# Routing a block every four to five shared-expert chunks and moving five blocks' shared products into the last stage of a ViT-tower kernel

## The chip, the cores and the metric

One NeuronCore of one Trainium2 chip runs the whole program. The metric is the device time of one launch in microseconds, given as the median of several runs. TensorE is written PE below, VectorE DVE, ScalarE ACT, GpSimd POOL and SyncE SP; PEld is PE's loading of weights, which overlaps its products. A name with q (SPq, ACTq) is that engine issuing a DMA.

## The reference, cut to what matters

```python
h = tok(x, ...)                  # real 2-D FFT of 16x16 patches, projection, class token, positions
h = h + ssm(layernorm(h), ...)   # causal convolution of each channel with a kernel of 197 taps
h = h + ffn(layernorm(h), ...)
def ffn(x):                      # 64 images x 197 tokens, width D = 192
    gates, idx = top_k(softmax(x @ router_w), 2)     # 8 experts, 2 for each token
    gates = gates / sum(gates)
    routed = sum over the 2 experts of gate * (silu(x @ w_gate[e]) * (x @ w_up[e])) @ w_down[e]
    shared = (silu(x @ ws_gate) * (x @ ws_up)) @ ws_down       # hidden width 768
    alpha = sigmoid(x @ sg_w + sg_b)
    return alpha * shared + (1 - alpha) * routed
```

All is float32 outside. Inside, the products of the FFN are made of float16 halves: each number is the sum of a high half and a low half (scaled by 16 for the weights), and a product is three to five products of halves.

## The kernel before, in words

`build` (L1697) runs five stages, one after the other, with a barrier between each and the next: `embed`, `mix`, and the three of `feed_forward`: `shared_expert`, `routed_experts`, `combine`.

**embed** (L148) reads the pixels, makes the 12608 token rows, stores them in `resid` and keeps their norm in the tile `u`. Beside that it makes the taps of the convolution: DVE raises powers step by step (`chain` and `raised`, most of whose instructions stand at the helper's line L433) into the tiles `zq` (14 powers) and `zp` (15), and PE multiplies them (`tap_products`, L384) in groups 5 to 10 of the 16 groups of images. `zp` already has its power index innermost in memory; `zq` has the channel innermost, and PE's moving operand reads it with a permuted pattern.

**mix** (L627) is the convolution. Its result lies in `y`; the last part of it is stored to `mixed` in DRAM by ACT's queue as the stage ends (`y_stored`).

**shared_expert** (L747) works on 25 blocks of 512 tokens (the last has 384). Two things happen for each block.
- *Routing* of a block: `add` (DVE: `resid` plus `mixed` into `sums`, then norm statistics, L1164 to L1173), `rstd` (POOL, L1111 and L1113), `normal` (DVE, L1179), `x_high` (ACT, L1039), `x_low` (POOL, L1117 and L1118), `transposes` (PE, 12 products, L943), `x_out` (ACT, L1044 and L1048, into `xt`), `router` (PE, 20 small products, L955), `logits` (DVE, L1191 to L1212), `tanh` (ACT), `ranks` (PE, L965 and L967), `slots` (DVE, L1218 to L1248), `send` (POOL, 8 indirect DMAs that scatter the token rows to `routed` by expert, L1128).
- *Shared products* of a block: six chunks m = 0..5 of 128 hidden units. For a chunk PE does `up` (10 products of 512 columns, L978, into `psg` and `psu`), ACT `silu` (L1059), DVE `hidden` (L1299), ACT `high` (L1067), DVE `low` (L1306), PE `down` (12 products of 192 columns, L992). After the six, DVE adds the block to `sums` (`token_out`, L1313).

The order on every engine is written out by hand in `body` functions. PE does `up` of a chunk and then `down` of the chunk two before it; both `psg`/`psu` and the hidden tiles have two buffers, so `up` of chunk c waits for `hidden` of c-2, and `down` of c-2 for `low` of c-2. Block b+1 is routed while block b's products run, each step at a fixed chunk of b: DVE has `add` at m = 0, `token_out` and `normal` at m = 1, `logits` at 4, `slots` at 5; ACT `x_high` at 2, `x_out` at 3; PE `transposes` at 3, `router` at 4, `ranks` at 5. `transposes` waits for `x_low` (and for `slots` of the block before). The FFN weights come in 12 pieces (`stage_in` on SP, `stage_high` on ACT, `stage_low` on DVE): four ahead of the first block, three in block 0, five in the last two. SP's queue starts with seven loads of constants (L877), then two pieces, then waits for `y_stored` and loads blocks 0 and 1 (one `hin` and four `yin` DMAs each). After the last block DVE works out the table of units (`unit_table`, L1250), and SP then stores eight blocks of filler rows at addresses that this table's first step gives (L925).

**routed_experts** (L1363) goes through 52 units of 512 rows. Its first load is SP's L1434, and its results are scattered to `parts`.

**combine** (L1640): for each block SP loads two parts (L1664), through a ring of six buffers; DVE adds one and then the other to `sums` (L1674, L1678); ACT's queue stores the block to `out` (L1694). PE and POOL do nothing.

Of the kernel before, what the change touches and what calls it, by code (L numbers as in the profile page):

```python
# [25 lines left out]
D = 192  # L26
# [52 lines left out]
NU = 60  # L79
MAX_UNITS = 2 * NTOK // UNIT + E  # L80
# [67 lines left out]
def embed(nc, io, u, area, taps, resid, mixed):  # L148

    with ExitStack() as ctx:  # L150
# [9 lines left out]
        zq, = pieces_of(free[1], ((2, KB, DH),))  # L160
# [112 lines left out]
        def _(act):  # L273
# [42 lines left out]
            for step in range(NG + 3):  # L316
# [56 lines left out]
        def _(pe):  # L373
# [11 lines left out]
            def tap_products(g, m):  # L385
# [325 lines left out]
def feed_forward(nc, io, area, y_stored, resid, mixed, routed, parts, out):  # L711

    with ExitStack() as ctx:
        t = {"w": [ctx.enter_context(nc.sbuf_tensor(f"ffn_w_{n}", [128, W_COLS], F16)) for n in ("hi", "lo")],
             "ident": ctx.enter_context(nc.sbuf_tensor("ident", [128, 128], F16)),
             "units": ctx.enter_context(nc.sbuf_tensor("units", [128, 2, NU], U32)),
             "expert": ctx.enter_context(nc.sbuf_tensor("expert", [128, NU], F32)),
             "pairs": ctx.enter_context(nc.sbuf_tensor("pairs", [128, 1], U32)),
             "sums": (ctx.enter_context(nc.sbuf_tensor("sums", [128, NTILE - HELD, D], F32)),
                      area[:, 0:HELD * D].rearrange("p (t d) -> p t d", d=D))}  # L720
        shared_expert(nc, io, t, area, y_stored, resid, mixed, routed, out)
        routed_experts(nc, t, routed, parts)
        combine(nc, t, parts, out)
# [23 lines left out]
def shared_expert(nc, io, t, area, y_stored, resid, mixed, routed, out):  # L747


    with ExitStack() as ctx:  # L750
# [7 lines left out]
        wa = [x[:, 0:2 * HS].rearrange("p (k h) -> p k h", k=2) for x in w]  # L758
        wb = [x[:, 2 * HS:4 * HS].rearrange("p (k h) -> p k h", k=2) for x in w]
        wd = [x[:, 4 * HS:W_SHARED].rearrange("p (m d) -> p m d", m=NSH) for x in w]  # L760
        wr = [sb(f"wr_{n}", [128, 2, E + 1], F16) for n in ("hi", "lo")]
        wrf = sb("wrf", [128, 2, E + 1])
        tri = sb("tri", [128, 128], F16)
        ones = sb("ones", [128, 128], F16)
        ids = sb("ids", [128, (NBLK + 1) * NT], U32)
        fields, width = table_fields()
        ctab = sb("ctab", [128, width])
# [6 lines left out]
        iota = sb("iota", [128, NT, E])  # L774
        sgb = sb("sgb", [128, NT, E + 1])
# [7 lines left out]
        LATER = {0: (4, 5, 6), NBLK - 2: (7, 8, 9), NBLK - 1: (10, 11)}  # L783

        def staged_at(b, m):

            late = LATER.get(b, ()) if isinstance(b, int) else ()
            return late[m // 2:m // 2 + 1] if m % 2 else ()

        hin = [sb(f"hin{i}", [128, NT, D]) for i in range(2)]  # L790
# [6 lines left out]
        rows_w = [sb(f"rows_w{i}", [128, NT, RX // 2], U32) for i in range(2)]  # L797
        xs = [x[:].bitcast(F16)[:, :, 0:XW] for x in rows_w]
        words = [x[:, :, XW // 2:RX // 2] for x in rows_w]
        fill = sb("fill", [128, NT, RX // 2], U32)  # L800
        xt = [sb(f"xt{i}", [128, 3, BT], F16) for i in range(2)]
# [8 lines left out]
        alpha = [sb(f"alpha{i}", [128, NT]) for i in range(2)]  # L810
# [9 lines left out]
        slot = [sb(f"slot{i}", [128, 2, NT], U32) for i in range(2)]  # L820
# [7 lines left out]
        ge = sb("ge", [128, NU, E + 1])  # L828
        gj = sb("gj", [128, NU, E + 1])
# [15 lines left out]
        names = ("const_in", "mixed_out", "stage_in0", "stage_in1", "oh_ready", "rank_ps", "slots_ready",  # L845
                 "sent0", "sent1", "base_set", "table", "fill_ready", "base_ready", "fillers", "stage_hi", "stage_lo", "wrf_hi", "wr_ready", "memsets",
# [10 lines left out]
        def schedule(eng, body):  # L857

            for b in range(NBLK):
                body(b, b % 2, tiles(b), tiles(b + 1))  # L860

        def tiles(b):
# [962 lines left out]
```

## Time and profile before

| what | us |
|---|---|
| median of 3 runs | 1355.6 |
| lowest, highest | 1353.54, 1363.51 |
| the profiled execution's own time | 1354.41 |
| its span (first to last instruction) | 1352.6 |
| PE busy | 1059.3 (78%) |
| DVE busy | 981.4 (73%) |
| POOL busy | 670.1 (50%) |
| ACT busy | 544.6 (40%) |
| DMA moved | 198.1 MB, 146 GB/s over the span |

Busy time is the union of an engine's instructions. The clock of a stretch is what was granted to TensorE as a share of full speed: 1.00 is 2.4 GHz, 0.50 is 1.2 GHz. Times in the trace count from the start of the span.

### The profile page before, as it was taken

Reading aid. Unit: us, or ns where it says so; the run is one execution under the profiler, and the core shown is the slowest. Engines: PE = TensorE matmul, PEld = TensorE weight load, DVE = VectorE, ACT = ScalarE, POOL = GpSimd, SP = SyncE. Lnnn points to the kernel's source line nnn. Section 1 sums busy time; section 2 is a strip of 40 time slices with the busy share of each in tenths; the row PEclk is TensorE's granted clock in tenths of the full one; section 3 lists DMA queues with packets and bytes.
Section 4 is the critical chain, followed back from the end, with each engine's and each line's share of the span. In section 5 each row is a group of like instructions: output and inputs, shape, how many; then the busy total and the mean of one; then the engine's idle time right before and its main releaser. Section 6 shows DMA issues by size and latency. Waiting matters only on the chain. (4 is left out here: it accounts for less than half of the span.)

```text
span 1352.6 us, 27592 instructions
## 1 busy us (share of the span) xinstructions
PE 1059.3 (78%) x8823; PEld 726.2 (54%) x8824; DVE 981.4 (73%) x2944; ACT 544.6 (40%) x992; POOL 670.1 (50%) x712
## 2 busy tenths in 40 slices
PE   2667999565159999999999999984999999998000
PEld 2556777465126666666666666652666666665000
DVE  6999879221168787787887877883888888887265
ACT  1124556421144444434444444441655655555000
POOL 2347778100034645556546455540777777777100
PEclk9876999787679999999999999996999999999555
DMA  6447778598874332332323322154444444443599
GB/s 226 152 161 251 241 252 216 154 273 181 164 187 123 88 83 67 83 82 73 78 66 87 83 70 75 40 145 139 132 128 121 129 135 125 135 127 104 172 369 340
DMA packets 213258, 198.10 MB, mean 146 GB/s; under 512 B 69712, under 2 KB 192114, under 8 KB 212910
## 3 DMA queue, kind: packets, MB, share of 16 engines
q1 hardware_dynamic: 166904, 131.86, 35.5%
q0 software_dynamic: 19488, 39.17, 8.4%
q10 hardware_dynamic: 26774, 25.89, 7.0%
q8 instruction: 52, 0.85, 0.3%
q14 instruction: 40, 0.33, 0.1%
HBM read 123.58 MB, written 74.41 MB: 146 GB/s over the span
## 5 line engine op out<-in xcount | busy, mean ns | idle before, releaser
L1550 POOL DMA_INDIRECT parts<-unit_yu,unit_token x208 | 225.8, 1086 | 73.3 <-issue 73.0
L1128 POOL DMA_INDIRECT routed<-rows_w,slot x198 | 203.8, 1029 | 55.0 <-issue 54.7
L1059 ACT ACTIVATE sg<-psg 128x512 f32<-128x512 f32 (+1 forms) x150 | 89.2, 595 | 210.0 <-PE psg L978 209.9
L1299 DVE SCALAR_TENSOR_TENSOR hf<-psu,sg 128x512 f32<-128x512 f32 (+1 forms) x150 | 101.7, 678 | 75.7 <-PE psu L978 75.2
L992 PE MATMUL pso<-ffn_w_hi,hh 128*128 128x192 f16 x594 | 146.3, 246 | 4.1 <-DVE hl L1306 3.0
L992 PE MATMUL pso<-ffn_w_hi,hl 128*128 128x192 f16 x594 | 146.1, 246 | 0.0
L992 PE MATMUL pso<-ffn_w_lo,hh 128*128 128x192 f16 x594 | 146.1, 246 | 0.0
L978 PE MATMUL psg<-xt,ffn_w_hi 128*128 128x512 f16 (+1 forms) x450 | 145.6, 378 | 0.0
L978 PE MATMUL psu<-xt,ffn_w_hi 128*128 128x512 f16 (+1 forms) x450 | 145.4, 377 | 0.0
L414 PE MATMUL ps<-w_hi,xh 128*98 128x192 f16 x384 | 106.6, 278 | 46.3 <-POOL xl L336 46.3
L336 POOL TENSOR_TENSOR xl<-area,xh 128x784 f16<-128x784 f32 x48 | 89.7, 1894 | 78.2 <-ACT xh L286 78.2
L978 PE MATMUL psg<-xt,ffn_w_lo 128*128 128x512 f16 (+1 forms) x300 | 113.5, 378 | 0.0
L978 PE MATMUL psu<-xt,ffn_w_lo 128*128 128x512 f16 (+1 forms) x300 | 113.1, 377 | 0.0
L1306 DVE TENSOR_TENSOR hl<-hf,hh 128x512 f16<-128x512 f32 (+1 forms) x150 | 111.9, 746 | 0.3 <-ACT hh L1067 0.3
L415 PE MATMUL ps<-w_lo,xh 128*98 128x192 f16 x384 | 101.8, 265 | 0.0
L416 PE MATMUL ps<-w_hi,xl 128*98 128x192 f16 x384 | 101.7, 265 | 0.0
L1111 POOL TENSOR_TENSOR ve<-mv,eps 128x4 f32<-128x4 f32 (+1 forms) x25 | 4.9, 196 | 194.3 <-DVE mv L1173 194.3
L1067 ACT CAST hh<-hf 128x512 f16<-128x512 f32 (+1 forms) x150 | 91.2, 608 | 1.8 <-DVE hf L1299 1.0
L674 PE MATMUL conv<-toeplitz,u 99*64 99x196 f32 x384 | 55.9, 371 | 39.9 <-DMA toeplitz<-taps 39.9
L414 PEld LDWEIGHTS ps<-w_hi,xh 128*98 128x98 f16 x384 | 51.2, 133 | 64.7 <-POOL xl L336 30.7
L1514 ACT ACTIVATE unit_yu<-u_out,unit_gates 128x192 f32<-128x192 f32 x104 | 38.1, 418 | 117.1 <-DVE unit_gates L1595 114.2
L286 ACT CAST xh<-area 128x784 f16<-128x784 f32 x48 | 38.6, 843 | 111.4 <-DVE area L534 68.4
(219 smaller groups left out, 2865.5 us busy)
## 6 DMA issues: line engine op xcount, KB each, us to landing
unit_xu<-routed SPq DMA_DIRECT2D x53, 392.0 KB
area<-in_xa_dram SPq DMA_DIRECT2D x48, 392.0 KB, 4.6
area<-in_xb_dram SPq DMA_DIRECT2D x48, 392.0 KB, 5.8
part<-parts SPq DMA_DIRECT2D x48, 384.0 KB, 9.3
toeplitz<-taps SPq DMA_DIRECT2D x24, 600.2 KB
resid<-h ACTq DMA_DIRECT2D x32, 294.0 KB
hin<-resid SPq DMA_DIRECT2D x24, 384.0 KB
yin<-mixed SPq DMA_DIRECT2D x96, 96.0 KB
```

What stands on the lines that cost most here:

```text
L336: nc.gpsimd.tensor_tensor(xl[g % 2][:, c], xa[n % NSLOT][:], xh[g % 2][:, c], ALU.subtract).then_inc(s["xl_ready"], 1)
L414: nc.tensor.matmul(out, xh[i][:, c, t], w_hi[:, c], start=(c == 0), stop=False)
L415: nc.tensor.matmul(out, xh[i][:, c, t], w_lo[:, c], start=False, stop=False)
L416: nc.tensor.matmul(out, xl[i][:, c, t], w_hi[:, c], start=False, stop=False)
L978: last = nc.tensor.matmul(ps[:, m % 2, 0:n], wt[:, k, cols], xt[q][:, c, 0:n], start=(a == 0), stop=(a == 4))
L992: last = nc.tensor.matmul(o, hx[m % 2][:, ts], wd[k][:, m], start=(a == 0 and m == 0 and t % 2 == 0), stop=(a == 2 and m == NSH - 1), skip ...
L1059: nc.scalar.activation(sg[m % 2][:, 0:n], psg[:, m % 2, 0:n], ACT.Silu, scale=1.0 / SCALE).then_inc(s["sg_ready"], 1)
L1067: nc.scalar.copy(hh[m % 2][:, 0:n], hf[m % 2][:, 0:n]).then_inc(s["hh_ready"], 1)
L1128: nc.gpsimd.indirect_dma_start(out=routed[:, :], out_offset=bass.IndirectOffsetOnAxis(ap=slot[q][:, k, t:t + 1], axis=0), in_=rows_w[q][:, ...
L1299: ins = nc.vector.scalar_tensor_tensor(out=hf[i][:, 0:n], in0=psu[:, i, 0:n], scalar=1.0 / SCALE, in1=sg[i][:, 0:n], op0=ALU.mult, op1=ALU ...
L1306: nc.vector.tensor_tensor(hl[m % 2][:, 0:n], hf[m % 2][:, 0:n], hh[m % 2][:, 0:n], ALU.subtract).then_inc(s["hl_ready"], 1)
L1550: nc.gpsimd.indirect_dma_start(out=parts[:, :], out_offset=bass.IndirectOffsetOnAxis(ap=token[q][:, k:k + 1], axis=0), in_=y[q][:, k, :], ...
```

## The change

- **Pace of routing.** 25 phases take the place of the 25 blocks as the unit of the hand-written order. Phase p routes block p+1 and lasts 5, 5 or 4 chunks in turn (the last one 8). The chunks are counted through, c = 0..119, for blocks 0 to 19 only, so routing runs ahead of the products. `xt` and `alpha` get 8 buffers in place of 2, the scattered rows and their slots 3 in place of 2.
- **Places in a phase** (i is the chunk of the phase): PE `ranks` of block p at 0, `transposes` of p+1 at 2, `router` at 3. DVE `add` of p+1 at 0, `normal` of p+1 and behind it `slots` of p at 1, `logits` at 3, a weight piece at 3. ACT `tanh` of p at 0, `x_high` at 1, `x_out` at 2. POOL `rstd`, `x_low`, then all 8 `send`s of block p.
- **Weights.** Pieces 4 to 11 come one a phase, in phases 0 to 7. At the start DVE does piece 0, 1, `add`, piece 2, `normal`, piece 3; PE starts its first `up` when three pieces are there; SP loads block 0 ahead of pieces 2 and 3, block 1 behind them.
- **Constants** are loaded on ACT's queue during the last three steps of `embed`.
- **End of the stage.** The filler rows are cleared by POOL, and the filler stores and `unit_table` start at i = 2 of the last phase; `fill` and the table's scratch use the weights' staging tiles.
- **Last stage** (`finish` in place of `combine`): the 30 chunks of blocks 20 to 24 run on PE, ACT and DVE; POOL adds the two parts of a block; DVE adds the sum to `sums` once, one block for each chunk but the first two and those with a `token_out`. SP issues stores as well as loads, through a ring of five.
- **Taps.** `zq` gets the power index innermost, so PE reads it without a permutation, and DVE writes it with a step.

```diff
+NLATE = 5
+NOW = NBLK - NLATE
+PACE = [5, 5, 4] * ((NBLK - 1) // 3) + [8]
+XR = 8
...
-        zq, = pieces_of(free[1], ((2, KB, DH),))
+        zqd, = pieces_of(free[1], ((2, DH, KB),))
+        zq = zqd.rearrange("p k d b -> p k b d")[:, :, ::-1]
...
+                if step >= NG:
+                    for name in (("w_r", "ident", "tri"), ("iota", "sgb"), ("ids", "ctab"))[step - NG]:
+                        act.dma_start(consts[name][:], io[name][:]).then_inc(consts["in"], 16)
...
-                                            zq[part, k, ::-1, ch].rearrange("n b d -> n d b"),
+                                            zqd[part, k, ch].rearrange("n d b -> n (d b)"),
...
+            def body(p, at, n):          # PE
+                for i in range(n):
+                    c = at + i
+                    up(c)
+                    if c == 2:
+                        pe.wait_ge(s["stage_lo"], 4)
+                    if c >= 2:
+                        down(c - 2)
+                    if i == 0:
+                        ranks(p)
+                    if i == 2 and p + 1 < NBLK:
+                        transposes(p + 1, tiles(p + 1))
+                    if i == 3 and p + 1 < NBLK:
+                        router(p + 1, tiles(p + 1))
...
+            def body(p, at, n):          # DVE
+                r = p + 1
+                for i in range(n):
+                    c = at + i
+                    hidden(c)
+                    if c:
+                        low(c - 1)
+                    if c % NSH == 1 and c > NSH:
+                        token_out(c // NSH - 1)
+                    if i == 0 and r < NBLK:
+                        add(r, r % 2, tiles(r))
+                    if i == 1:
+                        if r < NBLK:
+                            normal(r, r % 2, tiles(r))
+                        slots(p, tiles(p))
+                    if i == 3 and r < NBLK:
+                        logits(r, r % 2, tiles(r))
+                    if i == 3 and staged_at(p):
+                        stage_low(staged_at(p))
+                    if i == 2 and r == NBLK:
+                        dve.wait_ge(s["fill_clear"], 1)
...
+                        unit_table()
...
+        @block.sync                      # finish
+            for b in range(NBLK):
+                if b >= RING:
+                    store(b - RING)
+                nt = tiles(b)
+                for k in range(2):
+                    at = k * NTOK + start(b)
+                    sp.dma_start(y[b % RING][:, k, 0:nt], parts[at:at + nt * 128].rearrange("(t p) d -> p t d", p=128)
+                                 ).then_inc(y_in[b % RING], 16)
...
+        @block.gpsimd
+            for b in range(NBLK):
+                i, nt = b % RING, tiles(b)
+                pool.wait_ge(y_in[i], 32 * (b // RING + 1))
+                nc.gpsimd.tensor_tensor(y[i][:, 0, 0:nt], y[i][:, 0, 0:nt], y[i][:, 1, 0:nt],
+                                        ALU.add).then_inc(pair_added, 1)
...
+        @block.vector
+            for c in range(CHUNKS):
+                hidden(c)
+                if c:
+                    low(c - 1)
+                if c % NSH == 1 and c > NSH:
+                    token_out(NOW + c // NSH - 1)
+                elif c >= 2:
+                    combine(done)
+                    done += 1
```

## Rows read from the trace of the kernel before

**Rows 1.** Windows by stage: stretch, its length, busy PE, PEld, DVE, ACT, POOL, PE clock, DMA share, GB/s.

```profile
389.50:909.60 520.10, 508.21 (x4166) 320.39 (x4163) 425.45 (x1615) 227.00 (x404) 283.28 (x319) 1.00 0.33 85
1268.30:1352.60 84.30, 0.00 (x0) 0.00 (x0) 47.63 (x52) 0.00 (x0) 0.00 (x0) 0.50 1.04 346
```

**Rows 2.** Timeline at a boundary of blocks: start, us, engine, line, operation, idle before.

```profile
559.73 0.38 PE L978 MATMUL psu<-xt,ffn_w_lo 128*128 128x512 f16 x1
...
560.52 0.69 DVE L1299 SCALAR_TENSOR_TENSOR hf<-psu,sg 128x512 f32<-128x512 f32 x1
...
560.93 0.38 PE L978 MATMUL psg<-xt,ffn_w_hi 128*128 128x512 f16 x1
...
563.96 0.38 DVE L1173 BATCH_NORM_AGGREGATE mv<-st 128x2 f32<-128x6 f32 x4
...
564.08 0.38 PE L978 MATMUL psg<-xt,ffn_w_hi 128*128 128x512 f16 x1
...
564.70 1.04 POOL L1113 TENSOR_TENSOR rs<-ve,mhalf 128x4 f32<-128x4 f32 x1
...
565.43 1.39 DVE L1313 SCALAR_TENSOR_TENSOR sums<-pso,alpha,sums 128x192 f32<-128x192 f32 x4
...
566.73 1.33 DVE L1179 TENSOR_SCALAR xn<-sums,mv,rs 128x192 f32<-128x192 f32 x4
...
569.75 1.16 POOL L1118 TENSOR_TENSOR rows_w<-xn,rows_w 128x512 f16<-128x512 f32 x1
...
570.96 0.84 PE L943 MATMUL psx<-ident,rows_w 128*128 128x128 f16 x12 [0.28 <-POOL rows_w L1118]
...
571.64 0.38 PE L978 MATMUL psg<-xt,ffn_w_hi 128*128 128x512 f16 x1
```

**Rows 3.** Waits from 395 to 905 us: us in total, times, longest.

```profile
PEld psx L943 <- POOL rows_w L1118: 12.7, 23, 1.5
```

**Rows 4.** Timeline of `slots` for the first block: its first and its last instruction.

```profile
389.17 0.16 DVE L1218 TENSOR_SCALAR ga<-th 128x8 f32<-128x8 f32 x1
...
391.35 0.17 DVE L1248 COPY ixf<-ixf 128x8 f32<-128x8 f32 x1
```

**Rows 5.** Costliest groups by line: busy us, mean ns, idle before.

```profile
L1128 POOL DMA_INDIRECT routed<-rows_w,slot x198 | 203.8, 1029 | 55.0 <-issue 54.7
```

**Rows 6.** Timeline where `x_low` on POOL and `low` on DVE meet.

```profile
881.63 0.91 POOL L1118 TENSOR_TENSOR rows_w<-xn,rows_w 128x384 f16<-128x384 f32 x1
...
881.77 1.31 DVE L1306 TENSOR_TENSOR hl<-hf,hh 128x512 f16<-128x512 f32 x1
```

**Rows 7.** Timeline of the start of `shared_expert`.

```profile
345.47 4.15 SPq L877 DMA_DIRECT2D ident<-in_ident_dram  x1
...
358.42 0.43 SPq L880 DMA_DIRECT2D hin<-resid  x1
...
375.23 0.95 DVE L1164 TENSOR_TENSOR sums<-hin,yin 128x768 f32<-128x768 f32 x1
...
389.46 0.59 PE L978 MATMUL psg<-xt,ffn_w_hi 128*128 128x512 f16 x1
```

**Rows 8.** Timeline of the end of `shared_expert` and the next stage's first load.

```profile
911.55 9.58 SPq L925 DMA_DIRECT2D routed<-fill  x8
...
925.92 0.41 SPq L1434 DMA_DIRECT2D unit_xu<-routed  x1
```

**Rows 9.** Windows, columns as in rows 1: PE idle after that stage, then its first products.

```profile
910.00:920.00 10.00, 0.00 (x0) 0.00 (x0) 6.35 (x24) 0.00 (x0) 0.00 (x0) 0.71 0.71 232
929.50:935.20 5.70, 4.87 (x22) 2.52 (x23) 0.82 (x2) 1.18 (x2) 0.00 (x0) 0.54 0.40 118
```

**Rows 10.** Groups by form in `embed`, columns as in rows 5: DVE writing `zp` and `zq`.

```profile
L433 DVE TENSOR_TENSOR u<-u 128x672 f32<-128x672 f32 x1 | 1.3, 1305 | 0.0
...
L433 DVE TENSOR_TENSOR u<-u 128x480 f32<-128x480 f32 x1 | 0.7, 651 | 0.0
```

**Rows 11.** Timeline of PE in `embed`: the taps' products of one group.

```profile
151.37 1.01 PE L390 MATMUL ps<-u 64*120 64x112 f32 x4
```

More of the change, by code:

```diff
@@ L744, in sums_runs, with shared_expert @@
     return runs
-def shared_expert(nc, io, t, area, y_stored, resid, mixed, routed, out):
+def shared_expert(nc, io, t, area, y_stored, resid, mixed, routed, out, consts):
     with ExitStack() as ctx:
@@ L1328, in stage_low @@
                                                op0=ALU.mult, op1=ALU.subtract).then_inc(s["stage_lo"], 1)
[L1330 to L1331 removed]
+            stage_low(0)
+            stage_low(1)
             add(0, 0, NT)
+            stage_low(2)
             normal(0, 0, NT)
+            stage_low(3)
             logits(0, 0, NT)
[L1335 to L1355 removed]
@@ L1363, in routed_experts @@
+            schedule(body)
+            low(NSH * NOW - 1)
+            token_out(NOW - 1)
 def routed_experts(nc, t, routed, parts):
@@ L1657, in _, with store @@
         def _(sp):
+            n = [0]
+            def store(b):
+                sp.wait_ge(all_added, b + 1)
+                for lo, hi, sums in sums_runs(t, b, tiles(b)):
+                    old = (NBLK - 1) * BT - LAST_START if b == NBLK - 1 else 0
+                    if old:
+                        sp.dma_start(out[LAST_START + old:LAST_START + 128], sums[old:128, 0]).then_inc(stored, 16)
+                        lo, sums = lo + 1, sums[:, 1:]
+                        n[0] += 1
+                    rows = out[start(b) + lo * 128:start(b) + hi * 128].rearrange("(t p) d -> p t d", p=128)
+                    sp.dma_start(rows, sums).then_inc(stored, 16)
+                    n[0] += 1
@@ new lines, in _ @@
+            for b in range(NBLK):
[6 more added lines that the diff above has]
+                                 ).then_inc(y_in[b % RING], 16)
+            for b in range(NBLK - RING, NBLK):
+                store(b)
+            sp.wait_ge(stored, 16 * n[0])
@@ new lines, in low, with token_out @@
+            def low(c):
+                i, n = c % 2, place(c)[2] * 128
+                dve.wait_ge(hh_ready, c + 1)
+                nc.vector.tensor_tensor(hl[i][:, 0:n], hf[i][:, 0:n], hh[i][:, 0:n],
+                                        ALU.subtract).then_inc(hl_ready, 1)
+            def token_out(b):
+                dve.wait_ge(down_ps, NSH * (b - NOW + 1))
+                for i in range(tiles(b)):
+                    sums = sums_at(t, b, i)
+                    last = nc.vector.scalar_tensor_tensor(
+                        out=sums, in0=pso[:, i // 2, (i % 2) * D:(i % 2 + 1) * D],
+                        scalar=alpha[b % XR][:, i:i + 1], in1=sums, op0=ALU.mult, op1=ALU.add)
+                    if i % 2 or i == tiles(b) - 1:
+                        last.then_inc(out_ready, 1)
@@ L1699, in build @@
+            low(CHUNKS - 1)
+            token_out(NBLK - 1)
+            for b in range(done, NBLK):
+                combine(b)
 def build(nc, io, out):
```

511 lines of the change are left out of this document (264 added, 247 removed).

## The prediction

> **What bounds the kernel now.** I read the windows by stage first. In `shared_expert`, 520 us from the first shared product to the last, PE is busy 508 us at clock 1.00, DVE 425 and POOL 283: PE bounds it [rows 1]. In `combine`, 84.3 us, no PE instruction runs and the DMA share is 1.04: transfers bound it [rows 1]. So the change takes work from PE where PE bounds, and gives it to a stage where PE stands idle. Three gaps lie around these stages, and there I read the timeline: PE's first shared product comes at 389.46, 44 us after the stage's first load [rows 7]; after the last one `unit_table` runs (24 DVE instructions in 10 us) [rows 9], the filler stores are issued until 921.13, and the routed stage's first load goes out at 925.92 [rows 8].
>
> The timeline at a boundary of blocks gives the unit of all that follows: two chunks' first products are 560.93 and 564.08, so a chunk costs PE 3.15 us [rows 2]. Transposes take 0.68 (570.96 to 571.64) [rows 2], `router` about 0.5 and `ranks` about 0.3. Check: 144 full chunks are 453, the last six (384 columns, scaled) 14, 24 routings 36, the waits of PE for `x_low` 12.7 [rows 3], clock ramp and drain 3.5: 519 of 520.
>
> **1. Shared products, first part.** 120 chunks stay: 378 us. 24 transposes and routers 29, 25 `ranks` 7.5, ramp and drain 3.5: 418 without waits. The question is what each phase waits for, since `transposes` has moved from chunk 3 to chunk 2, while its chain still begins at chunk 0. I work it out from the moment T when `psu` of the phase's first chunk is complete.
> - The chain. `hidden`, `low`, `add` with statistics: 3.82 (560.52 to 564.34). `rstd` ends at 565.74: 1.40 more, and in this time `hidden` and `low` of the next chunk fit. `normal`, `x_high`, `x_low`: 566.73 to 570.91, 4.18 [rows 2]. With the hand-overs, T+9.45. Before, `token_out` (565.43) stood in it as well and DVE entered late.
> - PE. Before, T was 560.11 (the product of 559.73) and the next `up` began 0.82 later [rows 2]. Now: T+0.82, `ranks` 0.3, two chunks 6.3: at T+7.4 PE stands at `transposes`.
> - So PE waits 2.05 us. The same sum for before gives 10.3 against 10.8, 0.5 us; measured are 12.7/23 = 0.55 [rows 3].
> - A second condition: `transposes` waits for `slots` of the block before, which now comes right behind `normal`. It takes 2.35 (389.17 to 391.52) [rows 4], so it ends at T+8.95 if nothing disturbs it. But `x_low` now runs on POOL in just that time. A `low` beside `x_low` took 1.31 where it takes 0.68 [rows 6]: it lost 0.6. `slots` meets both instructions of `x_low`. Bounds: nothing (2.05 us of wait) to its whole remaining time being pushed behind `x_low` (3.4). I take 2.6, nearest to the one collision that a row shows.
>
> 24 waits of 2.6: 62. In 8 phases `token_out` falls on chunk 0 or 1 (c = 19, 25, 43, 61, 67, 85, 103, 109) and lengthens the chain by some 1.2: 10. After a phase of 4, `logits` makes DVE 0.25 late, and a weight piece twice 1.35: 5. `unit_table`, a clump of some 7 us on DVE (6.35 busy in rows 9), falls in the last phase, of which two chunks' buffers hide about half: 3.6. Sum 498 against 520: **-22** where 30 chunks less would be some -90. POOL is the next limit: rstd, the wait for `normal`, `x_low`, 8 sends of 1.31 (1.03 plus 0.28 idle) [rows 5] make 16.5 us for a phase of 16.7 or 19.9, so it just fits. DVE has 14 to 15 us of work in them. The third row buffer takes the wait for sent rows away; none is in the waits now, so it counts nothing.
>
> **2. Start of the stage.** Seven constants are ahead of everything on SP's queue: the first issues at 345.0, `ident` alone holds it 4.15, block 0's rows are issued at 358.42 and used at 375.23, since DVE does four weight pieces first; from `add` to the first product are 14.2 us [rows 7]. Now the pieces issue first and the rows as soon as `y_stored` is there. The queue ran freely from about 356, so the rows leave at 357 to 359, land some 6 later, `add` is at 365, and the first product 11.5 later (no `logits`, `ranks` ahead of it): 376.5. **-13**; bounds -6 (the two big pieces hold the queue as `ident` did, and `store_mixed` delays the rows) and -17. The seven issues are now on ACT at the end of `embed`, about 0.4 each; two of them stand behind its last `normal`: +0.5, in part 5.
>
> **3. End of the stage.** `unit_table` and the fillers leave the tail. From the last product to the next stage's first load are 16 us [rows 1, 8]; what stays is `token_out` and the barrier, 2.3. The 12 filler stores need about 20 us from chunk 2 of the last phase, which has 28 left; sends and table are done by then. **-13.5**, bounds -9 (the stores end late) and -14.
>
> **4. Last stage.** PE: 24 chunks of 3.15 and 6 of 2.37 are 90 us. It starts at clock 0.50: the routed stage's first 5.7 us ran at 0.54 [rows 9], so +2.8. The tail behind PE: `hidden` to `down` of the last chunk 1.3, `token_out` 1.2, last add 0.8, store 3.5. Hidden beside it: loads and stores. They kept 84.3/25 = 3.4 us a block with six buffers [rows 1]; with five the same flow is 4.0, against a need of 3.8 a block (five in six chunks), so near, but a first wait of DVE costs only what two chunks' slack leaves. DVE has 13.7 us in 18.9, and POOL's 768-element add (scaled from 1.16 for 512 [rows 2], 1.7) collides as in rows 6. For both together I take 5; bounds 0 and 23 (each of 25 adds blocks DVE for a large part). Sum 90+2.8+6.8+5 = 104.6: **+20**, bounds +15 and +38.
>
> **5. `embed`.** DVE's write with a step costs 1305/672 = 1.94 ns an element, without 1.36 [rows 10]; with reads some 5200 elements of `zq` get 0.6 dearer, +3.1, in a stretch where DVE is the busiest engine. PE's four passes are 1.01 us a group, 24 groups [rows 11]; if the permuted read holds them they may lose up to half, if the weight load does, nothing: 0 to -12. I take -4, one sixth. Net **-1** (bounds -9, +4).
> The Trainium skill (SBUF — State Buffer, under "Door 1: The DMA port swizzle") says that steps beyond a 16-byte line pay a penalty; the two DVE rows agree, 1.94 against 1.36 ns; for PE's read no row shows it, and by the rule `embed` would be nearer to its lower bound.
>
> Sum: 1354.4 - 22 - 13 - 13.5 + 20 - 1 = **1325 us**. The profiled execution lies 1.2 under the median of 1355.6, within its spread, so the same number stands for the median.
>
> **The rivals.**
> - *`slots` waits out `x_low`* (0.17): the wait is 3.4, not 2.6, so +19: **1344**. For it: DVE's loss in rows 6. Against: that loss was 0.6, not the whole of `x_low`. The Trainium skill (SBUF — State Buffer, "SBUF: two separate sides") states this as a rule: DVE and GpSimd take their shared ports as an exclusive lock for a whole instruction. The row agrees in kind; by the rule this is the case.
> - *The last stage is held by POOL's adds and the ring* (0.12): +38 in part 4, **1343**. Against it: DVE's slack and the average need of DMA.
> - *Routing hides wholly* (0.08): if the chain finds more room, as before with 0.55 a phase, the 24 waits and the `token_out` cases go: 1325 - 49 - 10 = **1266**. Against it: the same chain, worked out for before, gave the measured wait.
> - *PE's clock falls at the waits* (0.08), the slower side. With PE idle from 909.6 on, the window to 920 has a mean of 0.71: the clock fell within it [rows 9]. Before, the waits at `transposes` were 1.5 us at most and the stage stayed at 1.00 [rows 1, 3]; now they are 2 to 4 us long, 24 times. If the clock falls in each, each costs what the start of the routed stage did, half of 5.7 us [rows 9]: +67, **1392**. It decides from the point at which a wait lets the clock go, which no row shows; half of the waits falling would be enough for 1358, no change.
> - *The change doesn't do what it says*: it is a static order, so only its parts can miss; no share.
>
> **How the numbers follow.** 0.55 for the forecast, whose own range is 1305 to 1345; the rest as given. The low end 1298 leaves out the case 1266, the high end 1352 takes in both of 1344 and leaves out 1392. About 1% (13.5 us) is what a measurement of this kernel can tell from no change. Faster by over 1% (under 1342): 0.50 of my case, half of the next two, all of 1266: 0.71. Slower by over 1%: 0.08. The rest, 0.21.
>
> **What would show it.** First shared product near 376; in a phase PE waits 2 to 3.5 us at `transposes` for `x_low` or `slots`, 55 to 75 us over the stage; first to last product of `shared_expert` near 498; the routed stage's first load within 3 us of the last product; last stage near 104 with PE busy most of it and DMA under its bound. The forecast falls if PE's wait a phase is under 1 us or over 3.5, if the granted clock drops inside `shared_expert`, or if the last stage exceeds 115 us.

## The result, and the profile after

The changed kernel took 1364.4 us (median of 8 runs, 1358.0 to 1374.2) beside 1359.5 us for the kernel before (8 runs): a ratio of 1.0058, 95% interval 1.003 to 1.0086. The 29 us less that were forecast (1354.4 to 1325) did not come; the time is 39 us over the forecast. A second comparison, later, gave 1359.2 against 1355.9, ratio 1.0024 (1.0001 to 1.0047). So there the change costs a few tenths of a per cent; on a third chip, on which every kernel is slower, it costs 2% (below).

Windows by stage of the profiled execution after (1364.2 us, span 1362.4), columns as in [rows 1]: from the first load of the shared stage to its first product, from there to its last product, and the last stage.

```profile
337.00:366.50 29.50, 1.93 (x31) 1.72 (x32) 9.71 (x19) 7.60 (x10) 4.31 (x8) 0.51 0.84 190
366.50:914.20 547.70, 459.56 (x3532) 283.39 (x3529) 411.58 (x1579) 197.34 (x346) 290.85 (x320) 0.90 0.35 92
1260.40:1362.40 102.00, 93.82 (x642) 57.56 (x642) 84.09 (x105) 31.95 (x60) 48.78 (x25) 0.97 0.92 287
```

The stage that holds 30 chunks fewer has become longer: 547.7 us where [rows 1] has 520.1. Its granted clock is 0.90 where it was 1.00. Everything around it went nearly as forecast:

| stretch | before | after | difference | forecast |
|---|---|---|---|---|
| start to the stage's first load | 345.0 | 337.0 | -8 | -1 |
| first load to first shared product | 44.4 | 29.5 | -15 | -13 |
| first to last shared product | 520.1 | 547.7 | +27.6 | -22 |
| last product to the routed stage's first load | 16.6 | 3.2 | -13.4 | -13.5 |
| routed stage | 342.3 | 343.0 | +0.7 | 0 |
| last stage | 84.3 | 102.0 | +17.7 | +20 |

The first line is not a firm number: in the control run of the same kernel below, the first load comes at 349.3, and in the other profiles with the new taps it comes at 337.9 to 350.5. The load of the routed stage, SP's timeline after, stands where [rows 8] has 925.92:

```profile
905.45 0.37 SPq L948 DMA_DIRECT2D routed<-stage  x1
917.42 6.03 SPq L1457 DMA_DIRECT2D unit_xu<-routed  x3
```

What holds the middle stage shows in the waits after, from 366 to 900 us (total, times, longest), where [rows 3] had 12.7 us in 23:

```profile
PE psx L962 <- DVE ixf L1269: 80.4, 24, 4.2
...
PE pso L1012 <- DVE area L1331: 4.2, 1, 4.2
```

`psx L962` are the transposes and `ixf L1269` is the last instruction of `slots`: in the 24 phases PE stands 3.35 us in the mean before its transposes, and it is `slots` that releases it. The timeline of one such wait:

```profile
567.60 0.16 DVE L1239 TENSOR_SCALAR ga<-th 128x8 f32<-128x8 f32 x1
...
568.62 0.67 POOL L1133 TENSOR_TENSOR rows_w<-xn,rows_w 128x256 f16<-128x256 f32 x1 [2.23 <-ACT rows_w L1056]
...
568.74 1.71 DVE L1258 TENSOR_TENSOR pick<-hot,rank 128x32 f32<-128x32 f32 x2
...
569.25 1.15 POOL L1134 TENSOR_TENSOR rows_w<-xn,rows_w 128x512 f16<-128x512 f32 x1
570.49 0.28 DVE L1261 TENSOR_REDUCE slotf<-pick 128x4 f32<-128x32 f32 x2
...
571.21 0.17 DVE L1269 COPY ixf<-ixf 128x8 f32<-128x8 f32 x1
...
571.52 1.44 PE L962 MATMUL psx<-ident,rows_w 128*128 128x128 f16 x12 [4.09 <-DVE ixf L1269]
...
572.76 0.63 PE L997 MATMUL psg<-xt,ffn_w_hi 128*128 128x512 f16 x1
```

Two things are to be seen. `pick`, a pair of instructions of 32 elements, takes 1.71 us and ends at 570.45, when the second instruction of `x_low` on POOL ends (570.40). `slots` takes 3.78 us from 567.60 to 571.38 where it took 2.35 in [rows 4]. And behind the wait PE is slow: the transposes take 1.44 us where [rows 2] has 0.84, and a product 0.63 where it has 0.38. The windows of 2 us around this wait and around two later ones show the granted clock (the third number from the end, before the DMA share):

```profile
566.00:568.00 2.00, 1.43 (x15) 1.02 (x12) 1.97 (x10) 0.28 (x1) 0.40 (x1) 1.00 1.01 206
568.00:570.00 2.00, 0.00 (x0) 0.00 (x0) 1.93 (x10) 1.55 (x3) 1.38 (x2) 0.90 0.01 1
570.00:572.00 2.00, 0.48 (x5) 0.51 (x6) 1.86 (x8) 0.00 (x0) 0.60 (x2) 0.50 0.00 0
...
574.00:576.00 2.00, 2.00 (x6) 0.76 (x5) 0.00 (x0) 0.99 (x3) 1.70 (x2) 0.50 0.29 100
576.00:578.00 2.00, 2.00 (x26) 1.51 (x25) 1.00 (x2) 0.24 (x1) 1.39 (x3) 0.89 0.20 71
578.00:580.00 2.00, 2.00 (x24) 1.05 (x22) 1.77 (x17) 0.49 (x1) 1.70 (x2) 1.00 0.22 75
...
592.00:594.00 2.00, 0.00 (x0) 0.00 (x0) 1.86 (x7) 0.16 (x1) 1.01 (x1) 0.88 0.00 0
594.00:596.00 2.00, 1.87 (x14) 1.56 (x15) 2.00 (x5) 0.76 (x1) 1.39 (x2) 0.50 0.00 0
...
612.00:614.00 2.00, 0.67 (x9) 0.44 (x6) 1.90 (x11) 1.78 (x3) 1.14 (x2) 1.00 0.14 20
614.00:616.00 2.00, 0.24 (x5) 0.27 (x6) 1.86 (x7) 0.00 (x0) 0.83 (x2) 1.00 0.00 0
616.00:618.00 2.00, 2.00 (x19) 1.18 (x17) 0.84 (x2) 1.54 (x3) 1.32 (x1) 1.00 0.00 0
```

In the first two waits the clock falls to 0.50 (the 1.2 GHz level) and stays there for 3 to 5 us of work after the wait; in the third, with PE idle as long as in the second (3.09 and 3.02 us), it stays at 1.00 (2.4 GHz). Read off in such windows over the whole stage, the clock falls at 19 of the 24 waits, and once more behind `unit_table`. The Trainium skill (TensorE: Matmul & The Clock Gate, "HAM oscillation — how this bites in real kernels") describes just this pattern, a kernel that falls back at a wait in every turn of its loop and pays the slow start each time; the trace agrees, with the difference that here not every wait does it.

How much is which? PE's work of the stage at full clock follows from [rows 1]: 508.2 us less the 30 late chunks (24 of 3.15, 6 of 2.37) is 418.4. Busy time over that is the price of the half clock, the rest of the stage is idle time. After: 459.6 - 418.4 = 41 us of half clock, and 547.7 - 459.6 = 88 us idle. The forecast of 498 was 418 and 80 of waits. So of the 50 us by which it missed the stage, 8 are the waits and 41 the clock, which is about 2 us for each of the 20 falls.

### The profile page after: what moved, and what is told of

The parts are those of the page before. It is cut to its first block and busy times, and to the rows that moved or that the text cites. A ratio compares the mean times of both kernels' runs of the same rounds, so it can differ in the third digit from the quotient of the medians.

```text
span 1362.4 us, 27631 instructions
## 1 busy us (share of the span) xinstructions
PE 1101.0 (81%) x8823; PEld 745.2 (55%) x8824; DVE 999.6 (73%) x2918; ACT 545.2 (40%) x992; POOL 726.2 (53%) x737
## 5 line engine op out<-in xcount | busy, mean ns | idle before, releaser
L1319 DVE SCALAR_TENSOR_TENSOR hf<-psu,sg 128x512 f32<-128x512 f32 x120 | 82.1, 684 | 112.6 <-PE psu L997 106.8
L1077 ACT ACTIVATE sg<-psg 128x512 f32<-128x512 f32 x120 | 71.6, 597 | 184.0 <-PE psg L997 184.0
L997 PE MATMUL psg<-xt,ffn_w_hi 128*128 128x512 f16 x360 | 131.1, 421 | 0.0
L997 PE MATMUL psu<-xt,ffn_w_hi 128*128 128x512 f16 x360 | 126.7, 408 | 0.0
L1012 PE MATMUL pso<-ffn_w_hi,hh 128*128 128x192 f16 x480 | 119.0, 248 | 6.6 <-DVE area L1331 4.2
L1012 PE MATMUL pso<-ffn_w_lo,hh 128*128 128x192 f16 x480 | 118.8, 248 | 0.0
L962 PE MATMUL psx<-ident,rows_w 128*128 128x128 f16 x297 | 30.4, 276 | 109.0 <-DVE ixf L1269 80.4
L997 PE MATMUL psg<-xt,ffn_w_lo 128*128 128x512 f16 x240 | 100.4, 419 | 0.0
L997 PE MATMUL psu<-xt,ffn_w_lo 128*128 128x512 f16 x240 | 96.7, 403 | 0.0
L962 PEld LDWEIGHTS psx<-ident,rows_w 128*128 128x128 f16 x297 | 25.1, 125 | 113.9 <-issue 92.6
L1324 DVE TENSOR_TENSOR hl<-hf,hh 128x512 f16<-128x512 f32 x120 | 81.9, 682 | 0.3 <-ACT hh L1083 0.3
```

What stands on the lines that cost most here:

```text
L962: last = nc.tensor.transpose(o, xs[b % NR][:, t, c * 128:(c + 1) * 128], ident[:])
L997: last = nc.tensor.matmul(ps[:, m % 2], wt[:, k, cols], xt[b % XR][:, x], start=(a == 0), stop=(a == 4))
L1012: last = nc.tensor.matmul(o, hx[m % 2][:, ts], wd[k][:, m], start=(a == 0 and m == 0 and t % 2 == 0), stop=(a == 2 and m == NSH - 1), skip ...
L1077: nc.scalar.activation(sg[c % 2][:], psg[:, c % 2], ACT.Silu, scale=1.0 / SCALE).then_inc(s["sg_ready"], 1)
L1319: nc.vector.scalar_tensor_tensor(out=hf[i][:], in0=psu[:, i], scalar=1.0 / SCALE, in1=sg[i][:], op0=ALU.mult, op1=ALU.mult).then_inc(s["hf ...
L1324: nc.vector.tensor_tensor(hl[c % 2][:], hf[c % 2][:], hh[c % 2][:], ALU.subtract).then_inc(s["hl_ready"], 1)
```

## The experiments

Every ratio is to the kernel before in the same set, on one chip. Ten of the kernels ran on two chips on which every kernel, the one before too, took 8 to 10% longer (before: 1487 us in the first two sets, 1469 in the last; 1356 to 1357 in the other two). Their profiles have waits of ACT and DVE that those of the other chips haven't, so for them only ratios to the kernel before are used.

### Control: the changed kernel again

> No edit: the changed kernel itself beside the next three, so that they are compared on one chip. Every theory: 1.003 to 1.009 of the kernel before.

1.0205 (1.0131 to 1.028) on a chip of the slower kind (before 1486.7 us): outside what was expected.

> No edit, for comparison with the next three on one chip. 1.003 to 1.009 of the kernel before if the chip is like that of the first measurement, 1.013 to 1.028 if it is like that of the earlier control.

1359.2 us, 1.0024 (1.0001 to 1.0047), just under the expected 1.003. In its profile the stage is 538.8 us with 451.0 busy: the idle time is again 88 us, the half clock costs 33 where it was 41. The clock falls at 16 of the 24 waits where it was 19. So between these two executions the number of falls differs and the idle time doesn't.

### Is it slots that PE waits for? Early release of the transposes

```
-                    pe.wait_ge(s["slots_ready"], b)
+                    pe.wait_ge(s["rank_read"], b)
...
                 nc.vector.tensor_tensor(base[:], base[:], psx[:, 1, 384 + NT * E:384 + (NT + 1) * E], ALU.add
+                                        ).then_inc(s["rank_read"], 1)
```

> Edit: the transposes of a block wait for the last read of the ranks' bank by DVE (the sum into base) and no longer for the end of slots. Theory A, PE's wait at the transposes is ended by slots, which x_low on POOL has slowed (80.4 us in 24 waits): x_low is done about 1.1 us before slots, so 24 x 1.1 = 26 us go and the time is near 1338; the wait is then put down to POOL's x_low. Rival B, x_low ends at about the same time and slots was only the later of two: under 8 us go, 1356 to 1364.

0.9977 (0.9942 to 1.0012), on a chip of the slower kind. Beside that kind's control of 1.0205 it gains about 2%, but the two stand on different chips. The same edit beside the changed kernel on one chip:

> Edit as in the first experiment (the transposes wait for DVE's last read of the ranks' bank, not for the end of slots), now with the changed kernel beside it on the same chip. Theory A (slots, slowed by x_low, ends the wait): 26 to 44 us less than the changed kernel. Rival B: less than 8 us less.

1337.4 us, 0.9853 (0.9817 to 0.9889): 22 us less than the control beside it, a little under Theory A's 26 and far over Rival B's 8. The wait at the transposes in this kernel:

```profile
PE psx L962 <- POOL rows_w L1134: 92.7, 25, 28.7
```

Its window from the first to the last product of the stage:

```profile
371.50:891.90 520.40, 447.06 (x3532) 276.48 (x3529) 410.70 (x1579) 196.82 (x346) 292.94 (x320) 0.93 0.36 96
```

The releaser is now POOL's `x_low`. Without the first wait (28.7 us, before block 0) 64 us in 24 remain, 2.67 us a phase. Idle time is 73 us (520.4 - 447.1) against 88, half clock 29 against 33. So the end of `slots` was the later condition and cost 15 us of idle time; the chain to `x_low`, which I had put at 2.05 us, is 2.67 in this kernel.

### Does the half clock cost by itself? Products in the wait

```
                     if i == 2 and p + 1 < NBLK:
+                        for _ in range(12):
+                            nc.tensor.matmul(psx[:, 0], wa[0][:, 0, 0:128], xt[c // NSH % XR][:, 0],
+                                             start=True, stop=True)
                         transposes(p + 1, tiles(p + 1))
```

> Edit: 12 products of 512 columns into the transposes' own bank (overwritten by them) stand ahead of each wait at the transposes, 2.6 us of PE work at full clock in a wait of 3.35 us; the waits stay as they are. Theory A, a large part of the loss is the half clock behind each wait (transposes 1.44 in place of 0.84 us, the next chunk's products at 0.43 us each in place of 0.22), about 2 us in 24 phases: near 1364 - 48 = 1316, with the granted clock near 1.00 all through the stage. Rival B, the clock costs nothing, since DVE and POOL set the pace of a phase anyway: 1360 to 1366 with the clock at 1.00.

1.0064 (1.0043 to 1.0084) on a chip of the slower kind; the control's 1.0205 comes from another such chip. There the products did not hold the clock: it is 0.92 in the stage (371.9 to 993.6), PE is busy 521.1 us, and after the 62 us of the added products and the 418.4 of the stage's own work 41 us of half clock are left. The same edit on a chip of the other kind:

> Edit: only the 12 products of 512 columns ahead of each wait at the transposes; the transposes wait for the end of slots as in the change. Theory A (the half clock costs by itself: PE was busy 460 us in the stage for 418 us of work at full clock): the granted clock in the stage is near 1.00 and 25 to 42 us go, 0.973 to 0.985 of the kernel before. Rival B (a phase is bound by the chain through DVE, ACT and POOL, and PE at full clock only waits longer): 0 to 12 us go, 0.995 to 1.006.

1335.9 us, 0.9842 (0.979 to 0.9894): Theory A, at the edge of its range. The changed kernel itself did not run on this chip; the nearest to it there, the one with the old taps' layout (below), took 1362.3, 26 us more. Groups by form, a form of the stage's own products and the added ones:

```profile
L997 PE MATMUL psg<-xt,ffn_w_hi 128*128 128x512 f16 x360 | 118.7, 384 | 0.0
...
L1036 PE MATMUL psx<-xt,ffn_w_hi 128*128 128x512 f16 x288 | 66.1, 379 | 0.0
```

The window from the stage's first to its last product:

```profile
369.10:881.60 512.50, 482.32 (x3817) 294.41 (x3814) 410.59 (x1579) 195.37 (x346) 292.63 (x320) 0.99 0.37 97
```

The mean product is 384 ns where the changed kernel has 421, the clock is 0.99, and the stage is 512.5 us. PE's busy time less the 62 us of the 288 added products (0.215 each) is 420: no half clock is left. Its idle time and the added products together are 92 us, 4 more than the idle time before. So of the 33 to 41 us of half clock 26 to 35 come back, and little of it turns into waiting. This is the direct measure of the term that the forecast lacked: work that computes nothing makes the kernel 1.8 to 2.1% faster than its own ratios of 1.0024 and 1.0058.

> Edit: both, with 8 such products in place of 12. Theory A: the two savings add, 1364 - 26 - 48 = 1290. Rival B, one of them only uncovers the other bound (POOL's sends or DVE): within 10 us of the better of the two single edits.

0.9835 (0.9787 to 0.9883), 0.014 or 22 us under the early release alone on the same chip. Neither theory has that: the two savings did not add to the 1290 (0.949) of Theory A, and the gain is over the 10 us of Rival B.

> Edit: the same, with 12 products of 512 columns ahead of the wait. Theory A (the half clock behind the wait is a cost of its own): 20 to 40 us less than the early release alone; with 12 in place of the 8 of before the products reach nearly to the end of the wait, so that it is no more than 10 us from that run's distance to the kernel before (0.9835). Rival C (12 are more than the wait holds, each costs its 0.22 us): 10 to 20 us over the run with 8.

1328.0 us, 0.9783 (0.9741 to 0.9825), 9.4 us less than the early release alone. Theory A's lower bound of 20 is missed. The stage's profile says why: 504.2 us, no half clock, but 84.5 us of idle time and added products against 73 of idle time without them. Waits were 2.67 us in the mean and the products 2.58, so that in 11 of 24 phases no wait was left and they ran over. Rival C's mechanism holds in part; its number, 10 to 20 us over the run with 8, does not (0.9783 beside 0.9835).

### Place of the transposes or length of the phase?

```
-NLATE = 5
-PACE = [5, 5, 4] * ((NBLK - 1) // 3) + [8]
+NLATE = 1
+PACE = [6] * 18 + [5] * 6 + [6]
```

> Edit: one late block in place of five, so 144 chunks in 25 phases of 6 (six of 5); the places of all steps within a phase stay (transposes behind chunk 2 of it). Theory A, the wait and the half clock come from the place of the transposes two chunks after the chain begins, whatever the length of the phase: the stage keeps them and grows by 24 x 3.15 = 76 us, the last stage is some 14 us shorter (84 to 88 us): near 1426. Rival B, they come from phases of 4 to 5 chunks, in which DVE and POOL have too little time: with 6 the waits are near those of before, and what is left is the gain of start, end and embed: 1359.5 - 8 - 15 - 13 + 3 = 1326.

1.086 (1.0821 to 1.0899) on a chip of the slower kind: slower than the control of that kind, where Rival B has 0.975.

> Edit: one late block, phases of 6 chunks (six of 5), all places within a phase as in the change. Theory A (place): the waits of 3.3 us and the half clock stay in 24 phases, near 1359 + 76 - 14 = 1421, 1.048 of the kernel before. Rival B (length of phase): near 1326, 0.975.

1423.5 us, 1.0495 (1.0435 to 1.0554), 2.5 us from Theory A's number. The wait at the transposes, then the window of the stage:

```profile
PE psx L962 <- DVE ixf L1269: 84.8, 24, 4.3
```

```profile
367.40:982.20 614.80, 524.70 (x4060) 328.30 (x4056) 444.33 (x1643) 223.30 (x394) 287.69 (x320) 0.93 0.31 81
```

With as many chunks a phase as before, less six, the waits are the same 24 of 3.5 us, and the idle time is 90 us. The kernel before had 12.7 us of these waits with phases of 6. So it isn't the tighter pace but the places within the phase: `transposes` at chunk 2 with `slots` right ahead of it, while the chain still begins in chunk 0. The runs do not separate these places from one another here; the early release above gives 15 us of the idle time to `slots`. The clock costs 524.7 - 418.4 - 24 x 3.15 = 31 us.

With `NLATE = 4` and all phases of 5:

> Edit: four late blocks in place of five, all phases 5 chunks long (the last 6). The places of all steps within a phase stay. Theory A (wait and half clock hang on the transposes' place, two chunks behind the start of the chain): the stage keeps its 24 waits and grows by 6 x 3.15 = 19 us, the last stage loses 6 x 3.15 to 3.5 = 17 us or less: within 6 us of the changed kernel. Rival B (the phases of 4 chunks are what is too short): the waits fall and it is 20 us or more faster than the changed kernel.

1.0299 (1.0251 to 1.0348) beside the control's 1.0205 on the same chip, with intervals that overlap, and medians of 1525.8 and 1526.8 us: no gain from longer phases, as Theory A has it.

### A version that starts the chain earlier

If the place is the reason, the chain should start earlier. `add` goes to the last chunk of the phase before, `normal` and `x_high` to chunk 0, `rstd` between the sends, with four late blocks and phases of 5:

```
+                    if i == n - 1 and r + 1 < NBLK:
+                        add(r + 1, (r + 1) % 2, tiles(r + 1))
...
                 for t in range(tiles(p)):
+                    if t == 3 and r + 1 < NBLK:
+                        rstd(r + 1, tiles(r + 1))
                     send(p, t)
```

> Edit: as with four late blocks, and the chain begins one chunk earlier (add in the last chunk of the phase before, normal and x_high in chunk 0, rstd between the sends); slots and transposes stay at chunks 1 and 2. Theory A: x_low and slots end before PE comes to the transposes, the 3.35 us of wait and the 2 us of half clock behind it go in 24 phases, less about 1 us a phase for DVE, which then is nearly the bound: 24 x 4.3 = 103 us less than with four late blocks, near 1265 or 0.93 of the kernel before. Rival B (POOL's sends or DVE bound the phase): at most 30 us less, and the waits turn up at other instructions. Theory C (my own forecast of a wait of 2.6 us and no clock loss): 60 us less.

0.9934 (0.9896 to 0.9972), 46 us under the version with four late blocks and the old chain on the same chip (1525.8): half of what A has, over B's 30, nearest to the 60 of Theory C.

> Edit: the same, and the transposes wait for DVE's last read of the ranks' bank in place of the end of slots. Theory A: slots ends near the transposes' time with the chain ahead, so a few tenths of a us a phase are left to gain: 0 to 15 us less than without it.

0.9616 (0.9562 to 0.967): 48 us less again, where 0 to 15 were expected. The expectation was wrong. In the profile of the run before `slots` still ended waits at the transposes (26.4 us in 22), which is about half of it; here 0.6 us of them are left. The half clock in the stage goes from 50 us to 27 (busy 487.5 and 464.5, over 418.4 and the six added chunks), which is as large as the rest. Both are rough, since the earlier profile's execution took 1492.7 us beside a median of 1479.6.

> Edit: chain one chunk ahead and early release as before, but with the change's own pace of 5, 5 and 4 chunks and five late blocks. DVE then has add, logits and the next hidden in the last chunk of a phase of 4. Theory A (with the wait gone DVE bounds a phase, some 16.5 us for each of the 25, whatever the chunks): no faster than the same with four late blocks (0.9616 of before), 0.96 to 0.98. Rival B (PE still bounds): 19 us less work in the stage, 17 more in the last: 0.96.

1327.8 us, 0.9782 (0.9739 to 0.9825), 31 us under the control on that chip and in Theory A's range of 0.96 to 0.98.

> Edit: four late blocks, all phases 5 chunks, chain one chunk ahead, transposes released by the last read of the ranks' bank. Theory A (with both reasons to wait gone, and DVE's 16.4 us of work a phase under PE's 17.2): PE waits about 1 us a phase, the stage is near 126 x 3.15 + 36 + 25 = 458 us, the last stage near 88: 1275 to 1300, 0.94 to 0.96. Rival B (DVE or POOL bound the phase in spite of it): as with the pace of 5, 5, 4, near 1325.

1325.8 us, 0.9741 (0.9683 to 0.9799): Rival B's number. PE's longest wait in the stage of this kernel, then its timeline around one such wait:

```profile
PE pso L1012 <- DVE hl L1327: 43.4, 27, 4.6
```

```profile
608.52 0.21 ACT L1071 ACTIVATE th<-z 128x8 f32<-128x8 f32 x1
...
613.49 0.83 ACT L1056 CAST rows_w<-xn 128x768 f16<-128x768 f32 x1 [4.76 <-DVE xn L1201]
614.23 0.59 ACT L1077 ACTIVATE sg<-psg 128x512 f32<-128x512 f32 x1
614.72 0.61 ACT L1083 CAST hh<-hf 128x512 f16<-128x512 f32 x1
614.85 0.69 DVE L1322 SCALAR_TENSOR_TENSOR hf<-psu,sg 128x512 f32<-128x512 f32 x1 [1.39 <-ACT sg L1077]
...
615.46 1.27 DVE L1327 TENSOR_TENSOR hl<-hf,hh 128x512 f16<-128x512 f32 x1
...
616.79 0.26 PE L1012 MATMUL pso<-ffn_w_hi,hh 128*128 128x192 f16 x1 [1.60 <-DVE hl L1327]
```

PE no longer waits at the transposes but at `down` for `hl`. The chain behind it: `x_high`, which I had put into chunk 0, stands on ACT for 4.76 us waiting for `normal`, and `silu` and `high` of the next chunk queue behind it; DVE's `hidden` waits 1.39 us for that `silu`, `low` follows, and PE. A second thing is in these rows: `low` takes 1.27 us, where it takes 0.68 without a neighbour, since `x_low` now stands on POOL in the same time (its rows at 614.41 and 615.04). The next pair of kernels puts `x_high` back into chunk 1, behind `silu` and `high`.

```
-                    if i == 0 and r < NBLK:
+                    if i == 1 and r < NBLK:
                         x_high(r, tiles(r))
```

> Edit: the version with four late blocks, chain ahead and early release, with x_high back in chunk 1 on ACT, behind silu and high. Theory A (x_high blocks ACT: silu begins 2.3 us late behind it in a phase, DVE's hidden and low and PE's down follow, and PE's 43 us of waits at down come from it): 25 to 50 us less than with x_high in chunk 0, 1275 to 1300, 0.94 to 0.96 of the kernel before. Rival B (DVE's work bounds the phase): 0 to 10 us less.

0.9457 (0.9426 to 0.9488), on the chip of the slower kind that the control and the version without the move had in an earlier set. It lies in Theory A's 0.94 to 0.96. That version has 0.9616: 0.016 or 23 us apart by the ratios, 42 us by the times, since the kernel before took 1487 us in that set and 1469 in this; the size of the gain is open between the two. PE's waits at `down` for `hl` are 33.1 us in 38 where that version has 70.8 in 53, but 32.5 us in 24 stand at the transposes now, for the sum into `base`. The granted clock in the stage is 0.99. The edit did two things at once, though. Here is `low`, in that version first, then in this one:

```profile
L1327 DVE TENSOR_TENSOR hl<-hf,hh 128x512 f16<-128x512 f32 x126 | 105.5, 837 | 0.3 <-ACT hh L1083 0.3
```

```profile
L1327 DVE TENSOR_TENSOR hl<-hf,hh 128x512 f16<-128x512 f32 x126 | 85.7, 680 | 0.3 <-ACT hh L1083 0.3
```

`low` takes 20 us less in all, since `x_low` comes later and no longer meets it. How much of the gain is ACT's order and how much is this, no run separates.

> Edit: the same with the change's own pace of 5, 5 and 4 chunks and five late blocks. Theory A with DVE next (16.4 us of work a phase, 14.1 us of PE work in a phase of 4): 1285 to 1310, 0 to 15 us over the version with four late blocks. Rival B: as with x_high in chunk 0, near 1328.

0.9448 (0.9399 to 0.9496), the same as with four late blocks: how many blocks stand in the last stage no longer matters between four and five, which Theory A has within its 0 to 15. These two beat the kernel before by 5.4% and the change by more.

### The taps' operand

```
-        zqd, = pieces_of(free[1], ((2, DH, KB),))
-        zq = zqd.rearrange("p k d b -> p k b d")[:, :, ::-1]
+        zq, = pieces_of(free[1], ((2, KB, DH),))
```

> Edit: zq has its old layout again (DVE writes without a step, the product of the taps reads with one); all else as in the change. Theory A (the product's read with a step was on PE's path in embed, 383 against 287 ns for each of 96): the first load of the shared stage comes 4 to 8 us later than in the change, 1363 to 1367. My forecast's term (-4 and +3.1 cancel): within 1 us.

1362.3 us, 1.0031 (1.0 to 1.0061), not to be told from the change, and so not enough to tell the two expectations apart either. The groups by form, of this kernel first, then of the changed one in its profiled execution:

```profile
L399 PE MATMUL ps<-u 64*120 64x112 f32 x96 | 24.7, 389 | 0.0
```

```profile
L400 PE MATMUL ps<-u 64*120 64x112 f32 x96 | 16.0, 287 | 0.0
```

The product is faster with the new layout: 287 ns, 318 in the control, against 389 here and 383 in the kernel before. What of it arrives at the end of `mix` one cannot see: the stage's first load comes at 349.1 here and at 349.3 in the control, but at 337.0 in the changed kernel's first profile. ACT does wait for these products; its waits in the first 250 us, in the first profile of the change and in the control:

```profile
ACT xh L293 <- PE ps L400: 26.4, 6, 4.8
```

```profile
ACT xh L293 <- PE ps L400: 36.7, 6, 10.6
```

The same kernel's granted clock from 40 us to the end of `embed` is 0.87 in the first and 0.80 in the second. So the clock in `embed` goes with a difference of 12 us between two executions, which hides the layout's own worth.

## Why the prediction was wrong

**Part 1, the shared products (-22, measured +27.6).** This is the step that failed, and within it one term: PE's half clock stood in the sum at nothing. It costs 41 us in the profiled execution and 33 in the control. I had it as the rival "PE's clock falls at the waits", with the right place and a price for each fall, and gave it 0.08, although its only row [rows 9] showed the clock falling in a PE pause, and nothing that I wrote spoke against it for waits of 2 to 4 us. Of that price (+67 if all 24 fall) 41 came: 19 of 24 waits let the clock fall, and a fall cost about 2 us where I had 2.85. With it the forecast would have been 1366. That the clock costs by itself is shown by the products in the wait: 26 to 35 us of the stage come back with every release left as it was.

**The waits (80, measured 88).** The total was near, its parts less so. The wait at the transposes is 3.35 us, not 2.6: the rival "`slots` waits out `x_low`", 3.4, is what happened. The rule that I cited for it, the Trainium skill's SBUF — State Buffer, "SBUF: two separate sides", says that VectorE, with two inputs in SBUF, and GpSimd, reading SBUF, hold their shared ports as an exclusive lock for a whole instruction; the row of `pick`, 1.71 us to the end of `x_low` where 0.29 is its time without a neighbour (the row at 617.79 of the version with the chain ahead), agrees. No run took `x_low` off POOL, so the lock is read from rows, not tried. The row that I held against it speaks for it: in [rows 6] `low` begins at 881.77 and `x_low` ends at 882.54, so only 0.77 us of `x_low` was left to wait for, and the 0.63 that `low` lost is nearly all of it. That it is `slots` that ends the wait is shown by the early release. On the other side I had 18.6 us for `token_out`, `logits`, weights and `unit_table`; beyond the 80.4 us at the transposes only 8 us of idle time are there.

**The chain.** T+9.45 against PE at T+7.4 gave 2.05 us; with `slots` out of the way 2.67 were measured, and for the whole stage 73 us of idle time where that bound gives 49 + 18.6 = 68. That the places within the phase and not the pace are the reason was in the sum, and the run with one late block bears it out.

**Part 2, the start (-13)**: -15 from first load to first product, in the control too (349.3 to 378.9). **Part 3, the end (-13.5)**: -13.4, although I had 28 us left for the stores from chunk 2 of the last phase, and six chunks of 3.15 are 19. **Part 4, the last stage (+20)**: +17.7; PE is busy 93.8 of 102 us and DMA at 0.92. The rival of a last stage held by POOL and the ring falls. **Part 5, `embed` (-1)**: -8 in one execution, +4 in the control, so not measured. PE's read with a step did cost: the product took 383 and 389 ns in the two profiles with it, 287 to 325 in those without. The Trainium skill (SBUF — State Buffer, "Door 1: The DMA port swizzle") has a penalty for each access that crosses to a new 16-byte line; these rows agree in kind. ACT and DVE wait for this product in `embed` (31 us in the first profile of the change, 52 in the control, 50 before), so it may be worth something there; what, stays open.

In all: parts 2 to 4 forecast -6.5 and gave -10.6 in the profile; part 1 missed by 50. One sum of the chances is off: 0.50, half of 0.17 and 0.12, and 0.08 are 0.725 for faster by over 1%, not 0.71.

## What to carry to other kernels

A wait that is put on PE costs more than its length: price the work behind it at half clock as well, and where a row shows one fall of the clock, give that case the chance that the row earns, not that of an oddity. When a step is moved earlier in a software pipeline, move the head of its chain by the same distance, and look at what the in-order engines then queue behind each wait (here `slots` ahead of PE's release, and `x_high` ahead of `silu`) and at what two engines then do at the same moment (`x_low` beside `slots` or `low`). A semaphore should be raised by the instruction that frees the resource, not by the last one of the routine.

## What the runs showed of the hardware that was not expected

- The clock's fall is not the same in each wait of the same kernel: PE idle for 4.1 us from 567.4 and for 3.0 from 591.1 it falls, for 3.1 us from 612.7 it does not. The five waits of the 24 without a fall are 2.3 to 3.1 us long; two of 2.54 us have one.
- Products that compute nothing, placed in the wait, hold the clock (0.99 in the stage) and pay for themselves: 288 products for 25 to 29 us. On a chip with the long waits described next they did not (0.92).
- On two of the chips a kernel takes 8 to 10% longer. The waits of the control's profile there, beside none in the profiles of the other chips:

```profile
ACT sg L1077 <- remote: 142.8, 28, 8.4
...
ACT unit_yu L1537 <- remote: 81.7, 25, 3.9
...
DVE lg L1211 <- remote: 74.6, 23, 6.4
```

They come at intervals of some 26 us in the shared stage and once for each two units in the routed one, on ACT and DVE at about the same time, and the early stages are as on the other chips. What they are was not settled. They weigh more on the changed kernel (1.0205 there, 1.0024 and 1.0058 elsewhere) than on the one before, and less on the version with the chain ahead and four late blocks (0.9616 there, 0.9741 elsewhere).
